# Router stage of a three-layer kernel: row transposes moved into the last down product, their copies all on ScalarE, and another order of the first shared tile's products

## What is computed

```
h      = rmsnorm(x) * rms_weight              # per row, 1024 wide
logits = h @ router_w                         # 1024 x 8
topv, topi = top_k(softmax(logits), 2)        # two experts per row, weights renormalised
moe    = sum over both experts of topv * (silu(h @ w_gate[e]) * (h @ w_up[e])) @ w_down[e]
sh     = (silu(h @ sw_gate) * (h @ sw_up)) @ sw_down      # the shared expert, all rows
x      = x + moe + sh
```

## Time and profile before

| | |
|---|---|
| runs | 632.35, 632.56, 633.47 us, median 632.56 |
| profiled execution | span 630.4 us from the first to the last instruction; its own time isn't listed apart, and the median of the runs is 2.2 us above its span |
| TensorE busy, mean granted clock | 609.7 us (97%), 0.997 |
| VectorE busy | 510.8 us (81%) |
| ScalarE busy | 422.5 us (67%) |
| GpSimd busy | 193.7 us (31%) |
| DMA | 177.91 MB, mean 282 GB/s |

### The profile page before, as it was taken

How to read it: one execution, slowest core, us unless ns; L and a number is a source line. 1 busy time by engine, 2 the same in 40 slices (tenths; PEclk the granted TensorE clock), 3 DMA queues, 4 the chain that set the end, 5 groups by cost and what they waited for, 6 DMA issues and landing times.

```text
span 630.4 us, 10595 instructions
## 1 busy us (share of the span) xinstructions
PE 609.7 (97%) x3611; PEld 476.4 (76%) x3625; DVE 510.8 (81%) x887; ACT 422.5 (67%) x558; POOL 193.7 (31%) x174
## 2 busy tenths in 40 slices
PE   7999999998999999999998999999999999999996
PEld 6778888887887444444556888898998989889775
DVE  5888888888787777889999569688796887968687
ACT  4998888889755989885565357558385573846630
POOL 2254446426000333426930220040330404214051
PEclk9999999999999999999999999999999999999998
DMA  8977785865246997936999558796876968769357
GB/s 329 418 296 303 305 308 235 314 266 193 101 153 263 412 353 307 385 122 253 392 366 418 224 224 299 242 379 230 304 290 235 373 224 320 280 246 365 120 172 271
DMA packets 31070, 177.91 MB, mean 282 GB/s; under 512 B 4064, under 2 KB 4064, under 8 KB 14784
## 3 DMA queue, kind: packets, MB, share of 16 engines
q1 hardware_dynamic: 25536, 158.64, 65.9%
q0 software_dynamic: 5504, 18.88, 8.2%
HBM read 154.30 MB, written 23.20 MB: 282 GB/s over the span
## 4 chain that ended last, share of the span: by engine, by line
PE 59%; DVE 16%; ACT 13%; issue 5%; DMA 4%; POOL 2%; SPq 0%; DVEq 0%; POOLq 0%; ACTq 0%
PE BK L2157 11%; PE BK L306 9%; PE BK L1886 8%; PE BK L2160 4%; ACT RA L1387 4%; ACT PR L1414 4%; PE BK L318 3%; PE BK L2127 3%; PE BK L312 3%; PE BK L313 3%; DVE WL L1033 3%; PE BK L2115 2%; PE BK L1831 2%; PE BK L2113 2%; DMA RX<-wbit 1%
## 5 line engine op out<-in xcount | busy, mean ns | idle before, releaser
L2157 PE MATMUL BK<-EX,WH 128*128 128x320 f32 x384 | 99.4, 342 | 0.0
L702 POOL TENSOR_TENSOR WL<-RC,WH 128x2048 fp32r<-128x2048 f32 x7 | 45.5, 6505 | 167.8 <-ACT WH L1590 167.8
L1033 DVE TENSOR_TENSOR WL<-RA,WH 128x2048 fp32r<-128x2048 f32 x40 | 89.4, 2285 | 9.0 <-ACT WH L1590 8.8
L2160 PE MATMUL BK<-EX,WL 128*128 128x160 f32 x336 | 79.2, 236 | 0.0
L1590 ACT ACTIVATE WH<-RA 128x2048 fp32r<-128x2048 f32 x40 | 73.6, 1906 | 0.3 <-PE BK L1929 0.2
L2157 PEld LDWEIGHTS BK<-EX,WH 128*128 128x128 f32 x384 | 69.2, 189 | 0.0
L2160 PEld LDWEIGHTS BK<-EX,WL 128*128 128x128 f32 x336 | 64.1, 191 | 0.0
L652 POOL TENSOR_TENSOR HB<-HB,ND (+2 forms) x26 | 28.6, 1119 | 100.5 <-DVE BH L919 99.8
L1486 ACT ACTIVATE RA<-RA,RT 128x2048 int16<-128x2048 f32 x22 | 43.7, 1998 | 3.3 <-DVE RT L849 2.1
L1695 ACT ACTIVATE HX<-SR 128x320 fp32r<-128x320 f32 x16 | 7.5, 472 | 57.1 <-DVE SR L1083 57.1
L1886 PE MATMUL BK<-TG,XQ 128*128 128x512 bf16 x189 | 42.1, 379 | 0.2
(11 more groups left out here) (331 smaller groups left out, 1668.4 us busy)
## 6 DMA issues: line engine op xcount, KB each, us to landing
RA<-wbit SPq DMA_DIRECT2D x54, 1024.0 KB, 6.5
RA<-wmoe SPq DMA_DIRECT2D x40, 1024.0 KB, 6.5
RC<-wmoe SPq DMA_DIRECT2D x20, 1024.0 KB, 7.6
rows<-ZERO POOLq DMA_DIRECT2D x40, 256.0 KB, 8.2
XG<-rows SPq DMA_DIRECT2D x10, 512.0 KB, 3.6
rows<-YS SPq DMA_DIRECT2D x9, 512.0 KB, 4.2
RA<-wqk SPq DMA_DIRECT2D x7, 640.0 KB, 8.0
RA<-wo SPq DMA_DIRECT2D x4, 1024.0 KB, 7.4
```

Of the source, the lines that this page charges most:

```text
L702: e.tensor_tensor(WL[2][:, at], RC[5][:, :], WH[2][:, at].bitcast(f32), ALU.subtract).then_inc(free_c[5], 1)
L1033: e.tensor_tensor(WL[m][:, q * RAW:q * RAW + RAW], RC[j][:, :], WH[m][:, q * RAW:q * RAW + RAW].bitcast(f32), ALU.subtract)\
L2157: mm = e.matmul(bank[GBK[f]][:, 0:2 * R], WH[m][:, at], EX[:, k, :, :].rearrange("p a b -> p (a b)"), start=k == 0, stop=k == KD - 1)
L2160: e.matmul(bank[GBK[f]][:, 0:R], WL[m][:, at], EX[:, k, 0, :], start=False, stop=False)
```

## The change

It moves instructions and takes others' place; the products computed are the same. On TensorE: `router_t(0)` stands ahead of `down_part(3, 0)`, `router_t(1)` between the two halves, `router_t(2)` after them. The banks of tile 2's transposes change from (2, 3) to (4, 5), those of tile 0, so they wait for the low copy and tile 0's H3T. The first tile's gate and up products are written out (`first_products`): low rows times WH, high rows times WH, then high rows times WL at the end, with logits(0) to (2) and `router_t(3)` after the gate's high weights, logits(3) after its low weights, and `logits_t` amid the up product. On ScalarE: all H3T copies, two per tile; `rows_hi(0)` and tile 0's copies come ahead of tile 1's scale; the last root and scale stand around the split of the first down chunk. On VectorE: no H3T copies, `rows_lo(0)` ahead of tile 2's norm, and the norm of tile 3 ahead of the split of gate chunk 1.

```diff
-HB3 = ((4, 5), (6, 1), (2, 3), (6, 1))
+HB3 = ((4, 5), (6, 1), (4, 5), (6, 1))
@@ VectorE @@
-            def router_evac(t):
-                e.wait_ge(s("h3t_pe"), 2 * t)
-                e.tensor_copy(H3T[t][:, 4:8, :], r3(bank[HB3[t][1]], 4)).then_inc(s("h3t_d"), 1)
...
                 second_residual(t)
-                if t == NT - 1:
-                    split(0, 0, (1,))
+                if t == NT - 2:
+                    e.wait_ge(s("h3t_a"), 2)
+                    rows_lo(0)
                 e.wait_ge(s("x3"), t + 1)
                 router_rows(t)
-            rows_lo(0)
-            router_evac(1)
-            router_evac(2)
+            split(0, 0, (1,))
             e.wait_ge(s("lg_pe"), 1)
             split(0, 1, (0,))
-            router_evac(3)
             e.wait_ge(s("lg_pe"), 2)
@@ ScalarE @@
             def router_evac(t):
-                e.wait_ge(s("h3t_pe"), 2 * t - 1)
-                e.activation(H3T[t][:, 0:4, :], r3(bank[HB3[t][0]], 4), ACT.Copy).then_inc(s("h3t_a"), 1)
+                for q in range(2):
+                    if t:
+                        e.wait_ge(s("h3t_pe"), 2 * t + q - 1)
+                    e.activation(H3T[t][:, 4 * q:4 * q + 4, :], r3(bank[HB3[t][q]], 4), ACT.Copy).then_inc(s("h3t_a"), 1)
...
-            router_rows(1)
-            split(0, None, (0,))
-            router_rows(2)
...
+            router_root(1)
+            rows_hi(0)
+            router_evac(0)
+            router_scale(1)
+            split(0, None, (0,))
+            router_root(2)
+            router_evac(1)
+            router_scale(2)
             e.wait_ge(s("d_pe"), 2 * NT)
             split(0, None, (1,), (0,))
-            rows_hi(0)
-            for q in range(2):
-                e.activation(H3T[0][:, 4 * q:4 * q + 4, :], r3(bank[HB3[0][q]], 4), ACT.Copy).then_inc(s("h3t_a"), 1)
+            router_evac(2)
+            split(0, None, (1,), (1,))
             router_root(3)
-            router_evac(1)
-            split(0, None, (1,), (1,))
+            split(0, None, (2,), (0,))
             router_scale(3)
-            router_evac(2)
-            split(0, None, (2,), (0,))
+            split(0, None, (2,), (1,))
             router_evac(3)
-            split(0, None, (2,), (1,))
@@ TensorE @@
-            for q in range(2):
-                down_part(3, q, 0, KB)
...
             def router_t(t):
                 e.wait_ge(s("h3"), t + 1)
-                if t in (1, 2):
-                    e.wait_ge(s("x3"), t + 2)
+                if t == 1:
+                    e.wait_ge(s("x3"), 3)
+                elif t == 2:
+                    e.wait_ge(s("et_lo"), 3)
+                    e.wait_ge(s("h3t_a"), 2)
                 elif t == 3:
-                    e.wait_ge(s("h3t_a"), 3)
-                    e.wait_ge(s("h3t_d"), 1)
+                    e.wait_ge(s("h3t_a"), 4)
...
             def logits(t):
-                e.wait_ge(s("h3t_a"), t + 2)
-                if t:
-                    e.wait_ge(s("h3t_d"), t)
+                e.wait_ge(s("h3t_a"), 2 * t + 2)
...
+            def first_products():
+
+                e.wait_ge(s("et_hi"), 3)
+                e.wait_ge(s("et_lo"), 3)
+                e.wait_ge(s("m_hi"), 2)
+                high_weights(0, 1, range(KD), True, False)
+                high_weights(0, 0, range(KD), False, False)
+                for t in range(NT - 1):
+                    logits(t)
+                router_t(NT - 1)
+                for q in range(2):
+                    e.wait_ge(free_c[q], 1)
+                    ins = low_weights(0, range(4 * q, 4 * q + 4), q == 1)
+                ins.then_inc(s("gate_pe"), 2)
+                logits(NT - 1)
+                e.wait_ge(s("m_hi"), 4)
+                high_weights(1, 1, range(KD), True, False)
+                logits_t()
+                high_weights(1, 0, range(KD), False, False)
+                for q in range(2):
+                    e.wait_ge(free_c[2 + q], 1)
+                    ins = low_weights(1, range(4 * q, 4 * q + 4), q == 1)
+                ins.then_inc(s("up_pe"), 4)
...
-            for t in range(NT - 1):
-                router_t(t)
+            router_t(0)
+            down_part(3, 0, 0, KB)
+            router_t(1)
+            down_part(3, 1, 0, KB)
+            router_t(2)
```

More of the change, by code:

```diff
@@ L282, in program @@
                   "rnd", "tern_a", "tern", "g_pe", "silu", "h", "hq", "ht_pe", "hqt", "d_pe", "x3", "sh_last",
-                  "h3", "h3t_pe", "h3t_a", "h3t_d", "lg_pe", "lgs", "lgt_pe", "pos_rd", "top", "e1", "pos_pe", "cnt", "slots", "scat", "pself", "zero",
+                  "h3", "h3t_pe", "h3t_a", "lg_pe", "lgs", "lgt_pe", "pos_rd", "top", "e1", "pos_pe", "cnt", "slots", "scat", "pself", "zero",
                   "dself",
@@ L2028, in routed_rows, with high_weights, low_weights @@
                     rows_t(q, XG, at)
[L2030 to L2040, removed]
-            tiles_first = []
+            tiles_first = []
+            def high_weights(m, row, ks, first, last):
+                for k in ks:
+                    ins = e.matmul(bank[m], EX[:, k, row, 0:P], WH[m][:, k * FE:k * FE + FE],
+                                   start=first and k == ks[0], stop=last and k == ks[-1])
+                return ins
+            def low_weights(m, ks, last):
+                for k in ks:
+                    ins = e.matmul(bank[m], EX[:, k, 0, 0:P], WL[m][:, k * FE:k * FE + FE],
+                                   start=False, stop=last and k == ks[-1])
+                return ins
+            def first_products():
[20 more added lines that the diff above has]
+                ins.then_inc(s("up_pe"), 4)
             def last_up():
@@ L2060, in tile @@
                 more = n < NS
-                waits(e, ("et_hi", t * 3 + 3), (free_c[0], gi + 1))
+                if n == 0:
+                    first_products()
+                else:
+                    waits(e, ("et_hi", t * 3 + 3), (free_c[0], gi + 1))
                 if not more:
                     waits(e, ("et_lo", t * 3 + 3))
-                for m in range(2):
+                for m in range(2 if n else 0):
                     if m and n == NS - 1:
@@ L2072, in tile @@
                                            for k in range(4 * q, 4 * q + 4)], q == 0)
-                        if n == 0:
-                            routing((m, q))
                     e.wait_ge(s("et_lo"), t * 3 + 3)
@@ L2077, in tile @@
                         .then_inc(s(("gate_pe", "up_pe")[m]), (2, 4)[m])
-                    if n == 0:
-                        routing((m, 2))
                 if n < NS - 1:
```

## The result

The changed kernel takes 633.31 us (median of 20 runs, 631.99 to 634.78) against 632.34 us for the kernel before in the same comparison (20 runs, 631.10 to 633.47): ratio 1.0016, 95% interval 1.0010 to 1.0022. It is slower by 0.97 us where 1.35 us faster was forecast, and it lies outside the range given (629.8 to 632.9). The profiled execution's span is 632.2 us against 630.4; its own time, 634.01 us, is among the longer ones.

A forecast was written before the change was run, and what follows sets the result against it. TensorE, busy 97% of the span, was taken as the bound. Gaps removed 2.45 us, switches saved about 0.3, new waits 1.3 and 0.1: 1.35 us off 632.56 gives 631.2 us, range 629.8 to 632.9.

The forecast's parts named there:

- TensorE, part by part: TensorE from the last down products to the third logits: moved transposes cost 0.85 us each, three logits end at 335.1.
- Both old gaps: TensorE waits of 0.72 us before the third row transposes and 1.73 us before the second logits; both forecast gone.
- The new wait: Fourth transposes wait for tile 3's scale, queued on ScalarE behind the first down chunk's split; 1.3 us of waiting forecast.
- What is L?: Landing time of the first down weight chunk, summed from bytes ahead and beside it at 0.42 MB per us: 333.3 us.
- The latency of the row: Profiled 9.5 us from the chunk's issue to landing; would put landing at 334.6 us and the gain at 0.1 us.
- the formula: Gain at the end of the up product is 334.67 minus the first down chunk's landing time, at most about 2.7 us.
- rival C: Gain given back whole: chunk latency stays 9.5 us or slightly more, landing 334.2 to 335.9, time 632.1 to 633.8; chance 0.21.
- The clock: Granted clock read as 1.00, the full 2.4 GHz, at the router's transposes, so not what the stage loses.
- A: The forecast case: waiting 0.3 to 2.2 us for the chunk takes part of the gain, time 630.2 to 632.1; chance 0.56.
- D: Slower: chunk lands after 335.94 us and ScalarE holds TensorE over 3.9 us; 635.6 us at the neighbour's latency; chance 0.04.
- Rival E: f32 transposes amid the down product drop the clock to 1.2 GHz, 9.5 us more, 641 us; chance 0.02.
- Passing through: Behind the first shared tile TensorE is busy 27.30 of 28.00 us, so its win reaches the routed tiles nearly whole.

The follow-up runs named there:

- The filled gap: Changed kernel plus six unused matmuls ahead of the fourth transposes: 632.93 us, ratio 1.0013 to the kernel before; repeated, 632.53 us, ratio 1.0004.
- the changed kernel's second comparison: The changed kernel run again unaltered beside the kernel before: 634.46 us (5 runs) against 632.17, ratio 1.0044.
- the kernel with late zeros: Changed kernel with the last 6 of 40 zero transfers issued only after the last down product: 633.18 us, ratio 1.0012 to the kernel before.
- n = 10 and 11: Changed kernel with tile 3's scale and copies ahead of the down splits, plus 10 or 11 idle ScalarE copies before that scale: 631.75 and 633.83 us.

## Why the prediction was wrong, by its own steps

- **TensorE, part by part: right.** Transposes at 313.60, 319.23 and 324.85; 0.88 and 0.87 us for the two between bf16 runs (313.60 to 314.48), 0.85 taken, so the switch that no row showed costs next to nothing. Both old gaps gone, and three logits end at 334.9 instead of 335.1.
- **The new wait: its place and cause right, its size short.** The chunk gated ScalarE, with the scale behind it, as written. The step that failed first is **What is L?**: 333.3 forecast, 334.2 measured. The issue (325.04 for 325.1), the first bytes (about 329.8 for 329.75) and the rate (0.42 MB per us) were right. The mis-sized term is the overlap with the chunks behind this one: I took 0.2 MB, and 0.51 MB of them moved before it had landed. The zeros beside it were 0.31 MB for 0.25. (1.05 + 0.51 + 0.31) / 0.42 = 4.45 us gives 334.2. The 16 parts of the chunk came in over 1.6 us, on average at 333.4, near my sum by bytes; but ScalarE waits for the last. That zeros standing unevenly on the engines spread them so is likely and not shown. The latency of the row, 9.5 us, was the better estimate; it came out as 9.2. That is 0.9 us, and the formula with it gives 334.67 - 334.2 = 0.5 us faster, where rival C begins. The second chunk came at 337.5 us instead of 335.9, which cost nothing here, since TensorE was later still.
- **The clock: the step that turned the sign in the traces.** I read clock 1.00 around gaps of 0.72 and 1.73 us and wrote that the clock isn't what the stage loses. I then forecast a longer gap, with up to 2.2 us in the range of A and 3.9 in D, and priced each at its own length. The measured one of 2.33 us took the clock down and cost 1.54 us more. 0.47 - 1.54 is 1.07 us slower; 0.89 was measured at the end of the up product. Of the 0.18 between them, 0.06 is a slip in the prediction's sum (6.05 + 1.84 + 6.2 is 14.09, not 14.15), 0.06 comes back since the last logits' copies are no longer late, and the rest is spread over the stage. No rival had this fall, and slower by over 0.2% had a chance of 0.06. Rival E had the clock fall from the transposes amid the down product, which it didn't: 22 down matmuls keep their 4.75 us (314.48 to 319.23, 320.10 to 324.85), and the clock is 1.00 from 323 to 337 us. Its argument misread a row, without harm: the 24 transposes run from 323.15 to 326.6 us, 3.5 us and not 3. Rival D put a loss of 1.27 us at a landing of 335.94; with the clock's 1.54 it is at 334.4.
- **In the medians the clock isn't the whole of it.** Of the 20 runs of the changed kernel, nine list a mean granted clock of 0.996 or less, lower than any listed run of the kernel before; their median is 633.56 us. Eight list 0.998 or more, so they hold no such slow stretch; their median is 633.09, still 0.75 over the kernel before, where the trace without the 1.54 us would be 0.65 under. The filled gap, at a clock of 1.00 in both profiles, was 0.9 and 0.2 over. So the fall turns the sign in the profiled executions; in the runs another 0.4 to 1.4 us is lost besides (1.4 by the eight, 0.9 and 0.4 by the filled gap against its traces), on few runs each, and no trace shows where.
- **Passing through: right.** 0.89 us at the end of the up product, 0.91 at the first routed tile.

Open is what that further loss is, why the changed kernel's second comparison came out at 2.3 us over and not 1.0, and why the kernel with the filled gap was 0.9 us over in its first one, where its trace puts it level with the kernel before. I argued that the transfer lands at different times in different executions. The four profiled executions with the changed order of transfers and splits don't bear that out: the latency was 9.2 to 9.4 us in each. What differs between the traces is the gather at the end (7.4 to 8.9 us in these four) and, by the listed clocks, whether the clock falls. Whether the change has a part in the gather, one or two traces of a kernel don't tell.

## What to carry to other kernels

An in-order engine that feeds the critical one should do what is ready, and what the critical engine will ask for next, before anything that waits for a transfer; of the wait ask who stands behind it, not only who waits. When a forecast leaves a longer gap on TensorE than any the trace has shown at full clock, the gap needs a second price, the slow stretch behind it. And where a change has parts, the one that removes the named wait may do most of the work alone.

## What the runs showed of the hardware

Gaps of 0.93, 1.73 and 2.13 us left the granted clock at 1.00 in the profiled executions; gaps of 2.33, 2.47, 2.70, 2.75 and 3.98 us were each followed by a stretch near 0.5 that lasted about 3 us and cost 1.5 to 1.6 us. In the kernel with late zeros two gaps of 0.88 and 1.80 us, 4.0 us apart, were followed by the same, and at n = 10 and 11 executions of one kernel differ in it by their listed clocks, so the length of one gap doesn't settle it. A 1 MB transfer issued behind a queue of 256 KB writes moved next to nothing for 4.8 us; its 16 parts then landed over 1.6 us, with 0.5 MB of the transfers behind it moved before the last part was in. With 6 of the 40 writes taken out of its way it landed after 6.0 and 5.3 us instead of 9.2.
